# A third of eight groups with copied columns in the first edge stage of a graph network, with the register loads moved ahead

## The reference

```python
# layer 0: message passing
msg_in = jnp.concatenate([x[src], x[dst], edge_attr], axis=-1)
h = jax.nn.relu(msg_in @ msg_W1 + msg_b1)
messages = h @ msg_W2 + msg_b2
aggregated = jax.ops.segment_sum(messages, dst, num_segments=x.shape[0])
...   # update of the nodes, layer norm
# layer 1: attention over the same edges
z = jax.nn.leaky_relu(x_l[src] + x_r[dst], NEG_SLOPE)
...   # softmax over the edges of a target
out = jax.ops.segment_sum(alpha[:, :, None] * x_l[src], dst, num_segments=n)
```

## Time and profile before

| | |
|---|---|
| time, median of 3 runs | 3791.6 us (3791.53 to 3792.68) |
| profiled execution, its time | 3790.6 us |
| its span, first to last instruction | 3788.8 us |
| busy in the span: TensorE, VectorE, ScalarE, GpSimd | 2952.5, 3118.5, 2821.3, 2822.8 us |
| indirect gathers, first edge stage (L1016) | 1469, 950 ns each |
| indirect gathers, second edge stage (L1028) | 1472, 950 ns each |
| granted TensorE clock, mean of the span | 0.888 of full speed |

### The profile page before, as it was taken

One profiled execution on the slowest core, in us unless ns is written; L12 is line 12 of the kernel. 1 busy time (PEld: TensorE's weight loads), 2 busy tenths in 40 slices (PEclk: granted clock), 3 DMA queues, 4 the chain that ended last, 5 costly groups with the idle time before them and its releaser, 6 DMA issues.

```text
span 3788.8 us, 90744 instructions
## 1 busy us (share of the span) xinstructions
PE 2952.5 (78%) x19656; PEld 2513.2 (66%) x19786; DVE 3118.5 (82%) x20049; ACT 2821.3 (74%) x17211; POOL 2822.8 (75%) x2992
## 2 busy tenths in 40 slices
PE   6788888888888788788867777777777777777776
PEld 5787877778877778787845555555555555555554
DVE  5677777777777777777659999999999999999997
ACT  4666666666666666666548888888888888888884
POOL 6777777777777777777767777777777777777775
PEclk8878787878787887878779999999999999999999
DMA  7455555555555555555443333333333333333332
GB/s 201 135 142 142 143 142 140 149 144 142 140 144 140 145 142 141 143 141 143 112 118 89 90 91 90 90 90 90 91 91 90 91 91 90 90 90 90 90 91 57
DMA packets 364600, 442.62 MB, mean 117 GB/s; under 512 B 174981, under 2 KB 221411, under 8 KB 364047
## 3 DMA queue, kind: packets, MB, share of 16 engines
q1 hardware_dynamic: 269535, 243.82, 22.3%
q0 software_dynamic: 94112, 192.73, 20.4%
q10 hardware_dynamic: 400, 0.20, 0.0%
HBM read 413.17 MB, written 23.28 MB: 115 GB/s over the span
## 4 chain that ended last, share of the span: by engine, by line
POOL 67%; issue 22%; PE 4%; DMA 4%; DVE 2%; ACT 1%; SPq 0%; DVEq 0%; ACTq 0%; POOLq 0%
POOL t_ring L1028 37%; POOL m_ring L1016 30%; DMA m_ring<-tab_a,src_t 3%; PE bank L1688 1%; PE bank L1664 1%; DVE m_pre L1771 1%; PE bank L1675 1%; DMA tab_a<-m_pre 0%; DVE lone L977 0%; PE bank L1693 0%; ACT m_hid L1719 0%; ACT lone L1731 0%; DMA t_ring<-tab_l,src_t 0%; PE bank L2445 0%; PE bank L1324 0%
## 5 line engine op out<-in xcount | busy, mean ns | idle before, releaser
L1028 POOL DMA_INDIRECT t_ring<-tab_l,src_t x1472 | 1399.1, 950 | 466.4 <-issue 447.6
L1016 POOL DMA_INDIRECT m_ring<-tab_a,src_t x1469 | 1399.5, 953 | 459.3 <-issue 446.8
L2529 ACT ACTIVATE lone<-X 128x4 uint8 x7360 | 740.0, 189 | 68.7 <-issue 63.2
L1688 PE MATMUL bank<-w,m_attr_t 128*128 128x128 f32 x3128 | 697.1, 350 | 6.9 <-ACT m_attr_t L1728 6.5
L1731 ACT ACTIVATE lone<-HT 128x4 uint8 x6080 | 621.4, 190 | 74.5 <-issue 60.5
L1664 PE MATMUL bank<-m_hot,m_hid 128*128 128x32 f32 x3128 | 482.2, 302 | 236.6 <-ACT m_hid L1719 230.8
L1664 PEld LDWEIGHTS bank<-m_hot,m_hid 128*128 128x128 f32 x3128 | 451.0, 222 | 289.7 <-ACT m_hid L1719 283.0
L1688 PEld LDWEIGHTS bank<-w,m_attr_t 128*128 128x128 f32 x3128 | 603.9, 240 | 48.2 <-DVE m_hot L1756 13.5
L1771 DVE TENSOR_TENSOR m_pre<-bank,m_ring 128x512 f32<-128x512 f32 (+1 forms) x391 | 255.9, 654 | 415.9 <-DMA m_ring<-tab_a,src_t 320.9
L1719 ACT ACTIVATE m_hid<-m_pre 128x512 f32<-128x512 f32 x391 | 246.0, 629 | 416.8 <-DVE m_pre L1771 366.2
L977 DVE COPY lone<-HT 128x4 uint8 x6080 | 496.4, 195 | 61.2 <-issue 58.5
(11 more groups left out here) (268 smaller groups left out, 5984.6 us busy)
## 6 DMA issues: line engine op xcount, KB each, us to landing
m_ring<-in_edge_attr_dram SPq DMA_DIRECT2D x390, 256.0 KB
t_rows<-dst_rows SPq DMA_DIRECT2D x196, 256.0 KB
m_rows<-dst_rows SPq DMA_DIRECT2D x196, 192.0 KB
t_ring<-tab_l,src_t POOLq DMA_INDIRECT x1472
m_ring<-tab_a,src_t POOLq DMA_INDIRECT x1469
m_win<-tab_b SPq DMA_DIRECT2D x391, 24.0 KB
t_win<-tab_r SPq DMA_DIRECT2D x391, 24.0 KB
tab_b<-n_b SPq DMA_DIRECT2D x47, 96.0 KB
```

The lines of the kernel that those rows point to most:

```text
L1016: pool.indirect_dma_start(out=r.got[u][0:rows, j, :], out_offset=None, in_=k.tab_a, in_offset=bass.IndirectOffsetOnAxis(ap=k.src_t[0:rows, ...
L1028: pool.indirect_dma_start(out=r.got[u][0:rows, j, :], out_offset=None, in_=k.tab_l, in_offset=bass.IndirectOffsetOnAxis(ap=k.src_t[0:rows, ...
L1688: pe.matmul(p_hid[q % 2][:, e], lhsT=attr_t[q % 2][:, e], rhs=k.w1[:, 2, :], start=True, stop=False)
L2529: late_move(k, loaded, lambda out, col: act.activation(out, col, ACT.Copy), s["t_pick_s"])
```

## The change

Three slots of each round are picked, 2, 5 and 7, from group 10 on; 143 groups in all. The 128 columns of a group are copied in the steps between it and the picked group before it: over three steps as 24 + 20, 24 + 20 and 20 + 20 (VectorE + ScalarE), over two steps, for slot 7, as 32 + 32. Each of these begins at a multiple of 16 bytes in `places`. They are copied two steps ahead of the group's own step, as before, so that VectorE copies 20 (ScalarE 20) in slot 0, 24, 24, 20 in slots 1 to 3, 32, 32 in slots 4 and 5, 24, 24 in slots 6 and 7. `lone` has three buffers and no longer two. `pick_columns` becomes `pick_load` and `pick_move`; the load stands at the start of VectorE's step, ahead of the masks, and on ScalarE ahead of the wait for the transposed attributes. SyncE fetches the indices of a group at the slot two groups before it; before the change it was five groups.

```diff
-V = 4
-PICKED = P // V
-BY_VECTOR = 16
+IN_ROUND = (2, 5, 7)
+COLUMNS = {2: ((32, 32), (32, 32)), 3: ((24, 20), (24, 20), (20, 20))}
+DEPTH = 3
...
-    return g % V == V - 1 and U <= g < k.groups - 1
+    return g % U in IN_ROUND and U <= g < k.groups - 1
+
+
+def being_picked(k, v):
+
+    for n, g in enumerate(picks(k)):
+        if 0 <= v + SOONER - (g - span(k, g) + 1) < span(k, g):
+            return n, g, v + SOONER - (g - span(k, g) + 1)
+    return None
...
+def pick_load(nc, eng, k, m, v, engine):
+
+    now = being_picked(k, v)
+    if now is None:
+        return None
+    n, g, i = now
+    if i == 0:
+        if n == 0:
+            eng.wait_ge(k.s_ht, k.n_ht)
+        eng.wait_ge(m["m_places"], n + 1)
+        if n >= DEPTH:
+            eng.wait_ge(m["m_hp"], picks(k)[n - DEPTH] + 1)
+    columns = COLUMNS[span(k, g)]
+    first = sum(a + b for a, b in columns[:i]) + engine * columns[i][0]
+    _, places = nc.values_load_multi_w_load_instructions(
+        k.places[n % 2][:, first:first + columns[i][engine]], engines=[eng.engine], min_val=k.ht_at,
+        max_val=k.ht_at + 4 * (k.N - 1),
+        skip_runtime_bounds_check_because="src names rows of the node features, as the gathers take it")
+    return n, first, places
+
+
+def pick_move(k, loaded, move, done):
+
+    if loaded is None:
         return
...
-                    if u % V == 2:
-                        fetch_picked(sp, k, s, t["src"], (g + 2) // V)
+                    fetch_picked(sp, k, s, t["src"], g + 2)
...
                         g = rnd * U + u
+                        loaded = pick_load(nc, act, k, s, g, 1)
                         after(act, s["m_attrp"], g + 1)
                         act.activation(attr_t[u % 2][:], p_attr[u % 2][:], ACT.Copy).then_inc(s["m_attr"], 1)
-                        placed(nc, act, k, s, g)
-                        pick_columns(nc, act, k, s, g, BY_VECTOR, PICKED - BY_VECTOR,
-                                     lambda out, col: act.activation(out, col, ACT.Copy), s["m_picked_s"])
+                        placed(act, k, s, g)
+                        pick_move(k, loaded, lambda out, col: act.activation(out, col, ACT.Copy), s["m_picked_s"])
...
                         g = rnd * U + u
+                        loaded = pick_load(nc, dve, k, s, g, 0)
                         hold(dve, r.s_in[u], n_in[u] * (rnd + 1))
...
-                        pick_columns(nc, dve, k, s, g, 0, BY_VECTOR, dve.tensor_copy, s["m_picked_v"])
+                        pick_move(k, loaded, dve.tensor_copy, s["m_picked_v"])
```

More of the change, by code:

```diff
@@ L944, in picked, with picks @@
 def picked(k, g):
-    return g % V == V - 1 and U <= g < k.groups - 1
-def placed(nc, act, k, m, g):
-    n, i = (g + SOONER + 1) // V, (g + SOONER + 1) % V
-    if i or not picked(k, n * V + V - 1):
-        return
[L954 to L957, removed]
+    return g % U in IN_ROUND and U <= g < k.groups - 1
+def picks(k):
+    return [g for g in range(k.groups) if picked(k, g)]
@@ new lines, in span, with picks_until, placed @@
+def span(k, g):
+    own = picks(k)
+    n = own.index(g)
+    return g - own[n - 1] if n else 3
+def picks_until(k, g):
+    own = picks(k)
+    return g - (own[0] - span(k, own[0])) if g >= own[0] else 0
+def being_picked(k, v):
[3 more added lines that the diff above has]
+    return None
+def placed(act, k, m, v):
+    now = being_picked(k, v + 1)
+    if now is None or now[2]:
+        return
+    n, g, i = now
+    act.wait_ge(m["m_ids"], 16 * (n + 1))
+    if n >= 2:
+        act.wait_ge(m["m_picked_v"], picks_until(k, picks(k)[n - 2]))
+        act.wait_ge(m["m_picked_s"], picks_until(k, picks(k)[n - 2]))
@@ L958, in placed @@
     act.activation(k.places[n % 2], k.ids[n % 2], ACT.Copy, scale=4.0, bias=float(k.ht_at)
                    ).then_inc(m["m_places"], 1)
-def pick_columns(nc, eng, k, m, g, first, many, move, done):
-    n, i = (g + SOONER) // V, (g + SOONER) % V
-    if not picked(k, n * V + V - 1):
-        return
[L967 to L978, removed]
+def pick_load(nc, eng, k, m, v, engine):
+    now = being_picked(k, v)
+    if now is None:
+        return None
+    n, g, i = now
+    if i == 0:
[11 more added lines that the diff above has]
+    return n, first, places
@@ L979, in pick_columns, with fetch_picked @@
+def pick_move(k, loaded, move, done):
+    if loaded is None:
+        return
+    n, first, places = loaded
+    for q, place in enumerate(places):
+        last = move(k.lone[:, n % DEPTH, first + q:first + q + 1].bitcast(U8),
+                    k.HT[:].bitcast(U8)[:, bass.ds(place - k.ht_at, 4)])
     last.then_inc(done, 1)
-def fetch_picked(sp, k, m, src, n):
-    g = n * V + V - 1
+def fetch_picked(sp, k, m, src, g):
     if not picked(k, g):
         return
[L987 to L990, removed]
+    n = picks(k).index(g)
+    if n >= 2:
+        sp.wait_ge(m["m_places"], n - 1)
+    if n:
+        sp.wait_ge(m["m_ids"], 16 * n)
```

11 lines of the change are left out of this document (6 added, 5 removed).

## The result

The changed kernel takes 3968.9 us (median of 4 runs, 3966.7 to 3977.8) and the kernel before 3792.0 us (3791.5 to 3792.7): a ratio of 1.047, 95% interval 1.045 to 1.049. That is 177 us slower, where 142 were forecast. The profiled execution took 3968.6 us, with a span of 3966.8.

A forecast was written before the change was run, and what follows sets the result against it. VectorE was to replace GpSimd as the first edge stage's bound: 29.55 + 5.3 + 0.1 - 1.5 + 6.5 + 0.6 = 40.6 us a round against 37.58. Over 47.75 rounds that is 142 us more, 3933 us; range 3800 to 4025 us.

The forecast's parts named there:

- The bound moves from GpSimd to VectorE: First edge stage: GpSimd's round falls to 36.3 us with 29 gathers, and VectorE at 40.6 us sets the end.
- VectorE's own round, 40.6 us: First edge stage: VectorE's time a round, whatever GpSimd does, rises from 29.55 to 40.6 us.
- 5.3 + 0.1 - 0.3 = 5.1: VectorE, us a round: 72 more copied columns 5.3, L1771 split into sum and copy 0.1, less 0.3 of overlap.
- 1.35, 1.60 and 2.10 us: VectorE's register loads in the first edge stage: predicted lengths for 20, 24 and 32 registers.
- the prediction's floor of 0.1 us: Register loads: fixed time of a load, to which 0.063 us a register on VectorE is added.
- 1.26, 1.90, 1.90 and 1.40: VectorE's masks in slots 2, 4, 5 and 6: later by these us behind bare loads, 6.5 us a round together.
- The load does not start under the chain: VectorE, slots 2, 4, 5, 6: the load does not begin before the last waiting operation has begun.
- the second rival: VectorE's loads start hidden under the chains in slots 2, 4, 5, 6; GpSimd stays bound, 3730 us; chance 0.11.
- The rest is covered: ScalarE (at most 40 us a round), TensorE (under 0.5 us more) and SyncE's index fetches add nothing to the time.
- case 1: First edge stage: VectorE is the bound, 142 us more, 3933 us, ends 3873 and 4043 us; chance 0.70.
- the fourth rival: VectorE's waits for TensorE stay beside the new work: +1.9 us a round, 233 us in all, 4024 us; chance 0.07.
- 6.5 + 0.6 - 1.5 = 5.6: VectorE's loads, us a round: masks later in four chained steps 6.5, other four steps 0.6, less 1.5 for idle and overlap.

The follow-up runs named there:

- 3: Changed kernel without register loads in the first edge stage, columns copied from fixed places on both engines; 3756.0 us, ratio 0.990.
- 7: Changed kernel without VectorE's register loads (it copies from fixed places), ScalarE's loads left where the change put them; 3755.3 us, ratio 0.990.
- 4: Changed kernel with VectorE's load for the next step behind the addition to the accumulator, ahead of the node work; 3927.0 us, ratio 1.035.
- 8: Changed kernel without ScalarE's register loads (it copies from fixed places), VectorE's loads kept in the changed place; 3942.8 us, ratio 1.040.
- 5: Changed kernel with VectorE's next-step load ahead of the node work and ScalarE's directly behind its own copies; 3872.7 us, ratio 1.021.
- 1: Changed kernel with both loads back at old places: VectorE's behind the masks, ScalarE's behind the attribute copy; 3913.7 us, ratio 1.033.
- 9: Changed kernel with only VectorE's load back behind the masks, ScalarE's left ahead of its attribute copy; 3861.6 us, ratio 1.018.
- 6: Changed kernel with VectorE's load halved, ahead of node work and between its columns, ScalarE's load behind its own copies; 3780.9 us, ratio 0.996.
- 10: Changed kernel with both engines' loads in two parts, and 24 of 64 columns on VectorE in short steps instead of 32; 3735.0 us, ratio 0.985.

## Why the prediction was right, and where its sum was short

**The bound moves from GpSimd to VectorE: shown.** VectorE's ten rounds, full but for 11.6 us of waits, GpSimd's waits for L1811 and L1796, and no wait for gathers at L1811 say it, and the kernels 3 and 7 show what decides it. The chain bears it out only in part: the prediction wanted it on VectorE, and TensorE has as large a share of it (20% against 16 + 3).

**VectorE's own round, 40.6 us: measured 40.5.** That is 41.62 us less the 1.16 us of waits for TensorE at L1811. The terms held one by one. VectorE's busy time rose by 5.0 us a round (27.8 to 32.8), where 5.3 + 0.1 - 0.3 = 5.1 stood. Loads take 1.35, 1.60 and 2.10 us in the records for 20, 24 and 32 registers, so the line through the earlier trace rows goes on straight. It does not go on downwards: the prediction's floor of 0.1 us is only where the line meets zero, and the load of a single register takes 0.56 us on VectorE:

```profile
L1037 DVEq TENSOR_LOAD <-flag_i x1: 557/557/557, 51.5 to 51.5; - x1
```

The Trainium skill, "Runtime: NRT & Kernel Launch", section "Instruction fetch mechanics", has some 200 ns a register, for the register loads that the runtime injects; by it 32 registers would be 6.4 us, an estimate that this trace does not bear out for loads from the core's own memory. The idle time ahead of the masks, averaged over the ten rounds slot by slot from the trace's records, is 1.29, 1.89, 1.81 and 1.32 us at slots 2, 4, 5 and 6, where 1.26, 1.90, 1.90 and 1.40 stood in the sum, and 1.0 us at the other four together (0.8 of it at slot 1), where 0.6 stood. Nothing is left ahead of the columns.

**The load does not start under the chain: shown, the second rival falls.** The loads' own records say it: in the ten rounds, every load of slots 2, 4, 5 and 6 begins within 0.1 us after the last waiting operation ahead of it has begun (L1455, L1471, L1484 and L1492), and the masks begin 0.05 us after the load has ended. Experiment 4 shows the same from the other side: where the sum ahead of it waited, the load began behind it and was bare. The rule of the Trainium skill, "Perfetto Trace Analysis", section "DVE / Act Engine Instruction", that the sequencer is ready for the next instruction once one is pushed to the wait queue, does not hold for a register load in this kernel.

**"The rest is covered": the step that failed.** The sum took VectorE's waits for TensorE as nothing (case 1) and had 1.9 us a round for them in the fourth rival. The ten rounds have 11.6 us. They are 41.62 us long and not 40.55 (the sum before rounding), and 47.75 x 1.07 = 51 us are missing in the forecast; take off 7 us, since a round of the whole stage is on average 3.9 us longer than before and not 4.04, and the 9 us given back at its end, and the 35 us are there. The step went engine by engine: ScalarE and TensorE have time to spare. They have, ScalarE is busy 30.5 us of 41.6. But its loads now stand bare ahead of the attribute copy (L1768, 47.5 us in ten rounds; L1728 in the earlier trace rows had none), the copy feeds TensorE's products, and these feed VectorE's sum. Three pairs of kernels that differ in ScalarE's loads alone bear this out. In us of a round, over the same 42 rounds of each trace:

| kernels | round | loads bare on VectorE | waits for TensorE at the sum |
| --- | --- | --- | --- |
| the change, then 8 | 41.78, 41.27 | 7.4, 7.4 | 1.19, 0.78 |
| 4, then 5 | 40.96, 39.57 | 5.1, 4.6 | 2.79, 1.69 |
| 1, then 9 | 40.31, 39.73 | 4.5, 4.5 | 2.89, 2.36 |

Most of each gain is in the last column. So ScalarE's loads account for 0.4 of the 1.2 us a round that VectorE waits in the changed kernel, and for 26 us of its time (8). The other 0.8 us a round, some 37 us over 47.75 rounds, are there without any load on ScalarE: that is the larger part of what the case had put at nothing, and what brings it was not taken apart. ScalarE's loads cost nothing between 3 and 7, where VectorE has slack, and their place 54 us between 4 and 5.

**Place and length are one term.** 6.5 + 0.6 - 1.5 = 5.6 us a round, 267 us, stood in the sum for the loads' bare time over the old kernel's. Most of it would have come with the old place too: there the longer loads are bare for 4.3 us (9) or 4.4 us (1) a round, against 7.3 after. The place alone is then some 3 us a round, 140 us; put back it gives 107 us (9), and 55 us where ScalarE's goes back as well (1), since VectorE's waits for TensorE rise from 1.2 to 2.3 and 3.0 us. The term has its right size in the changed kernel and can't be taken out of it at that price: what leaves a full engine turns in part into waits for the next one.

**What stays open.** Some rounds take 44 to 46 us where 41 is typical, and in one of them, shown below, L1811 waits 2.71 us for TensorE at half its clock. How much of the missing time is the clock's was not measured. Nor is it shown where the 0.8 us a round of waits for TensorE come from that stay without ScalarE's loads, or why of all kernels experiment 4 has the lowest clock and such long waits of ScalarE for TensorE.

## What to carry to other kernels

A register load is work of the engine's queue, here 0.06 us a register (from 8 to 32 of them; a single one took 0.56 us), that begins when the last waiting operation ahead of it has begun, and only work that is already queued and waits for nothing hides it: put it behind a long run of such work (its own copies, split in halves), never between a chain and what the chain releases. When work is taken off the bound, add up the next engine's round with its queue time, and then ask not who is full but who hands on delay to whom: ScalarE's bare loads, on an engine with time to spare, cost nothing while GpSimd was the bound, and 26 to 54 us once VectorE was.

## What the runs showed of the hardware that was not expected

**Gathers last longer beside VectorE's column copies.** In the 1.3 ms from 400 to 1700 us of experiment 3, the 368 recorded gathers in which at least eight of VectorE's column copies begin last 1017 ns on average, 81 of them over 1000 ns; the 406 in which none begins last 946 ns, and the median is 945 ns in both. A long gather also has room for more copies; counted by the copies in its first 0.9 us alone, the means are 1002 and 948 ns. It is a minority of long gathers, then, and not all of them. In ten rounds the kernel before has 950 ns as its mean, the changed kernel 973 and experiment 3 967, but experiments 1, 4, 6 and 9, with the same 200 columns on VectorE, have 949 to 954 (5 and 8 have 967 and 970), and 10, with fewer, 955. So the copies alone do not set the mean, and the cause is open. In experiment 3 it takes 25 us of the 61 that one gather less a round was to bring.

**TensorE's clock falls after its own gaps, and differs from kernel to kernel.** The granted clock in the stretches above was 0.80 before, 0.73 after, 0.71 in experiment 4, 0.77 in 7, 0.80 in 3 and 0.86 in 10. It has two levels, 1.00 and 0.50 in these rows of the kernel after (2.4 and 1.2 GHz), four microseconds each:

```profile
710.00:714.00 4.00, 2.65 (x24) 2.28 (x22) 4.00 (x30) 3.33 (x26) 2.99 (x4) 0.96 0.73 208
714.00:718.00 4.00, 2.49 (x12) 2.46 (x13) 3.09 (x29) 2.69 (x16) 3.09 (x4) 0.50 0.32 87
718.00:722.00 4.00, 4.00 (x22) 3.81 (x22) 1.56 (x5) 2.72 (x22) 2.00 (x3) 0.50 0.35 98
722.00:726.00 4.00, 4.00 (x21) 3.75 (x20) 3.17 (x28) 2.49 (x21) 2.53 (x3) 0.50 0.49 130
726.00:730.00 4.00, 4.00 (x21) 3.81 (x21) 3.07 (x27) 2.56 (x14) 3.09 (x4) 0.50 0.50 121
...
734.00:738.00 4.00, 3.22 (x28) 2.71 (x27) 2.60 (x31) 2.74 (x25) 1.76 (x2) 1.00 0.54 151
```

TensorE stands idle for 2.85 us from 712.7 on, waiting for ScalarE, then works at the lower level until about 730 and is busy in every microsecond of 718 to 730. VectorE's wait of 2.71 us for it lies in there, on its timeline:

```profile
720.05 0.69 DVE L1811 TENSOR_TENSOR m_pre<-bank,m_ring 128x512 f32<-128x512 f32 x1 [2.71 <-PE bank L1732]
```

A gap on TensorE can so come back as a wait for TensorE; how much of these 2.71 us is the gap itself and how much the lower level is not shown. A gap ahead of a fall is the usual order: cut into stretches of 2 us from 200 to 1800 us, the kernel after has some 60 falls to the lower level, and in the two stretches ahead of one TensorE is busy for 60% on average, against 89% ahead of stretches that stay at the upper level (56% and 87% in the kernel before). At the lower level it is busy 92% of the time, at the upper 79%. Still, only 17.2 of the 44.4 us that VectorE waits for it at L1811 in this time end at the lower level, and that level has 56% of the time. In 3 and 7, where GpSimd decides, the time is the same at 0.80 and at 0.77. So the clock may be one road on which the delay travels, these waits do not gather at its lower level, and its price in the changed kernel is open.
